# Running the first FFN inside the causal attention, four steps behind it, as one program

## The reference

```python
x = x + attn_a(layernorm(x))    # 16 heads of 8, causal; three heads weight a third of the keys by 1.6
x = x + ffn(layernorm(x))
x = x + attn_b(layernorm(x))    # 16 heads of 8, rotary q and k, no mask
x = x + ffn(layernorm(x))

# ffn: 128 -> 512 -> 512 -> 512 -> 128, ternary weights times a scale per row
h = silu(lin(x, w1)) * lin(x, w2)
h = gelu(lin(h, h1)); h = gelu(lin(h, h2)); y = lin(h, w3)
```

## Time and profile before

| what | us |
|---|---|
| median of 3 runs | 2510.14 |
| lowest and highest | 2504.98 and 2511.56 |
| profiled execution, its own time | 2512.21 |
| its span, first to last instruction | 2510.5 |

### The profile page before, as it was taken

One profiled execution on the slowest core, in us unless ns is written; L12 is line 12 of the kernel. 1 busy time (PEld: TensorE's weight loads), 2 busy tenths in 40 slices (PEclk: granted clock), 3 DMA queues, 4 the chain that ended last, 5 costly groups with the idle time before them and its releaser, 6 DMA issues. The chain is left out here.

```text
span 2510.5 us, 37314 instructions
## 1 busy us (share of the span) xinstructions
PE 2132.8 (85%) x13378; PEld 978.4 (39%) x13378; DVE 1729.4 (69%) x2590; ACT 1482.9 (59%) x2980; POOL 982.5 (39%) x1184
## 2 busy tenths in 40 slices
PE   0889999898996899999379889989998885999998
PEld 0323333233331677777112222222222211777776
DVE  5766777677670666665189899989989833667663
ACT  0265656666663556655127777777777772665655
POOL 2344555454542344554323232323323200544544
PEclk8688988889895899999659999999999986999999
DMA  6243534334331000000323423443343300000000
GB/s 172 64 99 66 114 69 93 85 79 103 66 66 20 1 1 1 1 1 1 75 51 66 104 64 66 88 89 66 67 104 67 66 15 10 8 10 14 13 10 17
DMA packets 99853, 136.48 MB, mean 54 GB/s; under 512 B 20560, under 2 KB 81488, under 8 KB 93520
## 3 DMA queue, kind: packets, MB, share of 16 engines
q1 hardware_dynamic: 99664, 134.02, 24.5%
HBM read 67.91 MB, written 55.57 MB: 49 GB/s over the span
## 5 line engine op out<-in xcount | busy, mean ns | idle before, releaser
L576 DVE TENSOR_REDUCE b_negmax<-ps_max 128x2 f32<-128x1024 f32 x512 | 611.5, 1219 | 97.5 <-PE ps_max L693 95.4
L660 ACT ACTIVATE b_prob<-ps_score 128x512 f32<-128x512 f32 x1024 | 547.7, 598 | 206.8 <-PE ps_score L679 205.6
L660 ACT ACTIVATE a_prob<-ps_score 128x512 f32<-128x512 f32 (+3 forms) x1024 | 384.5, 437 | 259.4 <-PE ps_score L679 256.8
L576 DVE TENSOR_REDUCE a_negmax<-ps_max 128x2 f32<-128x256 f32 (+3 forms) x512 | 410.9, 821 | 178.8 <-PE ps_max L697 173.6
L679 PE MATMUL ps_score<-b_stack_q,stack_k 50*128 50x512 bf16 x1024 | 263.5, 396 | 54.6 <-ACT b_prob L660 46.1
L714 PE MATMUL ps_out<-b_prob,b_v_aug 128*9 128x512 f32 x2048 | 277.7, 615 | 18.3 <-ACT b_o_raw L633 12.5
L493 POOL TENSOR_SCALAR_AFFINE_SELECT a_prob<-a_prob 128x512 f32<-128x512 f32 x256 | 162.5, 635 | 320.9 <-ACT a_prob L660 320.7
L974 PE MATMUL ps_score<-fb_h,w_hi 128*128 128x512 f32 x1024 | 251.9, 401 | 29.8 <-DVE fb_h L888 28.8
L974 PE MATMUL ps_score<-fa_h,w_hi 128*128 128x512 f32 x1024 | 251.5, 400 | 29.7 <-DVE fa_h L888 28.7
L693 PE MATMUL ps_max<-stack_k,b_stack_q 48*128 48x512 bf16 x1024 | 233.5, 396 | 40.6 <-issue 23.8
L679 PE MATMUL ps_score<-a_stack_q,stack_k 50*128 50x512 bf16 (+3 forms) x1024 | 202.2, 330 | 37.5 <-DMA a_stack_q<-a_nm_rows 30.6
(11 more groups left out here) (139 smaller groups left out, 2961.1 us busy)
## 6 DMA issues: line engine op xcount, KB each, us to landing
stack_k<-d_stack SPq DMA_DIRECT2D x64, 384.0 KB, 5.9
d_stack<-a_parts SPq DMA_DIRECT2D x64, 192.0 KB, 4.1
a_stack_q<-d_stack SPq DMA_DIRECT2D x32, 384.0 KB, 5.5
d_stack<-b_parts SPq DMA_DIRECT2D x64, 192.0 KB, 3.7
b_stack_q<-d_stack SPq DMA_DIRECT2D x32, 384.0 KB, 5.5
d_stack<-a_parts SPq DMA_DIRECT2D x64, 128.0 KB, 3.6
d_stack<-b_parts SPq DMA_DIRECT2D x64, 128.0 KB, 3.4
d_stack<-a_parts SPq DMA_DIRECT2D x64, 64.0 KB, 3.7
```

The source lines that it names most:

```text
L576: dve.tensor_reduce(m["negmax"][:, t, :, p], dve_banks("max", k)[:, :, 0:keys], AX.X, ALU.max, negate=True).then_inc(s["max"], 1)
L660: act.activation(m["prob"][u % PROBS][:, g, lo:S], act_bank("score", 4 * u + g)[:, 0:S - lo], ACT.Exp).then_inc(s["prob"], 1)
```

## The change

The causal attention and the first FFN become one stage, `layer`, with one loop of 20 steps. In step n the FFN works on batch n-4 (`FFN = 4`), whose attention ended in step n-1: the output projection moves one step up, to batch n-3 in unit 11. The FFN's work is put into units: turn of the norm in unit 0, gates in units 2 to 5, the hidden layers as blocks behind units 7 and 12, the output layer in unit 14 and its turn in unit 15. In the blocks no scores are made; a maximum stands after each slice. Outside them a unit has one maximum, in eight of the units two. A batch is no longer in its gates while another is in its hidden layers: one batch goes through all of the FFN in one step. The banks stay three and two pairs, and their turns now include the FFN's.

To make room in SBUF there are two stacks instead of three and three buffers of probabilities instead of four. The stacks are loaded in halves of four pairs of heads, the first as soon as the scores of the batch two steps before have passed that half. The gates' low parts go from DVE to POOL; the gates' products are made in place. Norm statistics and xhat of batch n+1 are made in units 10 and 13 of step n. The memsets that put ones into `stack_k` go from the setup into each attention stage. The rotary attention and the second FFN stay as they are but for that and for the flag and half scales, which are now made once, in `layer`. PE's program of the fused stage is written three times (steps 0 and 1, then with and without low weights from step 2).

Cut to its core:

```diff
...
+HALF_LOADS = 4 * 16
...
+SECOND_MAX = (7, 8, 9, 10, 12, 13, 14, 15)
+HIDDEN_UNIT = {2: 7, 3: 12}
+HIDDEN_MAXES = 4
+GATE_UNIT = (2, 3, 4, 5)
+SLOT = {"xT": 0, "fxT": 0, "q": 1, "nm1": 1, "k": 6, "v": 8, "nm0": 11, "proj": 11, "yT": 14, "y": 15}
+ROTARY_SLOT = {"nm1": 1, "xT": 3, "q": 4, "qr": 5, "k": 6, "kr": 7, "v": 8, "nm0": 10, "proj": 2}
...
+def first_max(u):
+    blocks = sum(HIDDEN_MAXES for at in HIDDEN_UNIT.values() if at < u)
+    return u + sum(1 for v in SECOND_MAX if v < u) + blocks
...
-        for stage in (lambda sem: attention(nc, sem, m, a, "a", causal=True),
-                      lambda sem: ffn(nc, sem, m, a, "fa", None),
-                      lambda sem: attention(nc, sem, m, a, "b", causal=False),
-                      lambda sem: ffn(nc, sem, m, a, "fb", out)):
+        for stage in (lambda sem: layer(nc, sem, m, a, "a"),
+                      lambda sem: attention(nc, sem, m, a, "b"),
+                      lambda sem: ffn(nc, sem, m, "fb", out)):
...
-            for c in range(STACKS):
-                last = dve.memset(m["stack_k"][c][:], 1.0)
-            last.then_inc(zeroed, 1)
...
+def layer(nc, sem, m, a, tag):
...
+    STACKS, PROBS, LAG = 2, 3, 2
...
+    act_turns, dve_turns = [], []
+    for u in range(UNITS):
+        act_turns += [("score", 2, 4 * u), ("score", 2, 4 * u + 1)]
+        dve_turns.append(("max", 1, first_max(u)))
+        if u == SLOT["xT"]:
+            act_turns.append(("xT", 0, 0))
+        if u == SLOT["fxT"]:
+            dve_turns.append(("fxT", FFN, 0))
+        act_turns += [("score", 2, 4 * u + 2), ("score", 2, 4 * u + 3)]
+        if u in GATE_UNIT:
+            dve_turns.append(("gate", FFN, GATE_UNIT.index(u)))
+        if u == SLOT["nm1"]:
+            act_turns.append(("nm1", 2, 0))
+        for name in ("q", "k"):
+            if u == SLOT[name]:
+                dve_turns.append((name, 0, 0))
+        if u == SLOT["v"]:
+            dve_turns.append(("v", 0, 0))
+        if u == SLOT["nm0"]:
+            act_turns.append(("nm0", 1, 0))
+        if u == SLOT["proj"]:
+            dve_turns.append(("proj", 3, 0))
+        if u == SLOT["yT"]:
+            act_turns.append(("yT", FFN, 0))
+        if u == SLOT["y"]:
+            dve_turns.append(("y", FFN, 0))
+        if u in SECOND_MAX:
+            dve_turns.append(("max", 1, first_max(u) + 1))
+        for k, at in HIDDEN_UNIT.items():
+            if u == at:
+                act_turns += [(f"h{k}", FFN, f) for f in range(FT)]
+                dve_turns += [("max", 1, first_max(u + 1) - HIDDEN_MAXES + i) for i in range(HIDDEN_MAXES)]
+    act_turns += [None] * (-len(act_turns) % SCORE_BANKS)
+    dve_turns += [None] * (-len(dve_turns) % 2)
...
+        elif name == "gate":
+            pe.wait_ge(s["h1f"], count(FT, b, k + 1))
...
+            for n in range(STEPS):
+                if on(n, 2):
+                    aug(1, n - 2)
+                if on(n, 3):
+                    numerators(n - 3)
+                if on(n, 0):
+                    store(n, "stored_q", 0)
+                if on(n, 3):
+                    store_reciprocals(n - 3)
+                if on(n, 0):
+                    store(n, "stored_k", 1)
+                if on(n, 3):
+                    spread_reciprocals(n - 3)
+                if on(n, 0):
+                    load(n, "stack_q", "stored_q", 0, 0)
+                    load(n, "stack_k", "stored_k", 1, 0)
+                if on(n, 1):
+                    aug(0, n - 1)
+                if on(n, 0):
+                    load(n, "stack_q", "stored_q", 0, 1)
+                    load(n, "stack_k", "stored_k", 1, 1)
...
+            def gate_low(b, f):
+                pool.wait_ge(s["h1_hi"], count(FT, b, f + 1))
+                pool.tensor_tensor(h[1][:, 1, f], gated[:, f % 2], h[1][:, 0, f], ALU.subtract).then_inc(s["h1"], 1)
+            def hidden_low(b, k):
+                for f in range(FT):
+                    pool.wait_ge(s[f"h{k}_hi"], count(FT, b, f + 1))
+                    pool.tensor_tensor(h[k][:, 1, f], hf[:, f % 2], h[k][:, 0, f], ALU.subtract)\
+                        .then_inc(s[f"h{k}"], 1)
...
+            def gate(b, f):
+                banks = dve_banks("gate", f)
+                dve.wait_ge(s["tanh"], count(FT, b, f + 1))
+                dve.scalar_tensor_tensor(out=gated[:, f % 2], in0=gated[:, f % 2], scalar=1.0,
+                                         in1=banks[:, 0], op0=ALU.add, op1=ALU.mult).then_inc(s["ut"], 1)
+                dve.wait_ge(s["ut"], count(FT, b, f + 1))
+                dve.scalar_tensor_tensor(out=gated[:, f % 2], in0=banks[:, 1], scalar=m["s_gate"][:, f:f + 1],
+                                         in1=gated[:, f % 2], op0=ALU.mult, op1=ALU.mult).then_inc(s["h1f"], 1)
+                dve.wait_ge(s["h1f"], count(FT, b, f + 1))
+                if f == 0:
+                    wait(dve, s["yT_ps"], b)
+                dve.tensor_copy(h[1][:, 0, f], gated[:, f % 2]).then_inc(s["h1_hi"], 1)
...
+            norm_stats(dve, m, s, 0, "")
+            for c in range(STACKS):
+                last = dve.memset(m["stack_k"][c][:], 1.0)
+            last.then_inc(s["unit_rows"], 1)
+            norm_apply(dve, m, s, 0, "")
...
+            def hidden(b, k):
+                for f in range(FT):
+                    act.wait_ge(s[f"l{k}_ps"], count(FT, b, f + 1))
+                    if f >= 2:
+                        act.wait_ge(s[f"h{k}"], count(FT, b, f - 1))
+                    elif k == 3:
+                        act.wait_ge(s["h2"], count(FT, b, f + 3))
+                    else:
+                        wait(act, s["h3"], count(FT, b - 1, f + 3))
+                    act.activation(hf[:, f % 2], act_bank(f"h{k}", f), ACT.Gelu, scale=m["s_col"][:, k, f:f + 1])\
+                        .then_inc(s[f"h{k}f"], 1)
+                    act.wait_ge(s[f"h{k}f"], count(FT, b, f + 1))
+                    if f == 0 and k == 2:
+                        wait(act, s["l3_ps"], count(FT, b))
+                    act.activation(h[k][:, 0, f], hf[:, f % 2], ACT.Copy).then_inc(s[f"h{k}_hi"], 1)
...
+                for n in range(first, end):
+                    for u in range(UNITS):
+                        if on(n, 2):
+                            scores(n, u, 0)
+                        if on(n, 1):
+                            maxes(n, first_max(u))
+                        attention_middle(n, u)
+                        if u == SLOT["fxT"] and on(n, FFN):
+                            pe.wait_ge(s["f_xhat"], n - FFN + 1)
+                            dve_banks_free(pe, n, "fxT")
+                            turn(dve_banks("fxT")[:, 0], lambda t: m["f_xhat"][:, t, :]).then_inc(s["f_xT_ps"], 1)
+                        if on(n, 2):
+                            scores(n, u, 1)
+                        if u in GATE_UNIT and on(n, FFN):
+                            gates(n, GATE_UNIT.index(u))
+                        attention_end(n, u)
+                        if u == SLOT["yT"] and on(n, FFN):
+                            output(n)
+                        if u == SLOT["y"] and on(n, FFN):
+                            pe.wait_ge(s["yT"], n - FFN + 1)
+                            dve_banks_free(pe, n, "y")
+                            turn(dve_banks("y")[:, 0], lambda t: yT[:, P * t:P * (t + 1)]).then_inc(s["y_ps"], 1)
+                        if u in SECOND_MAX and on(n, 1):
+                            maxes(n, first_max(u) + 1)
+                        if u < LAG and on(n, 3):
+                            weigh(n - 3, UNITS - LAG + u)
+                        if u >= LAG and on(n, 2):
+                            weigh(n - 2, u - LAG)
+                        for k, at in HIDDEN_UNIT.items():
+                            if u == at:
+                                for f in range(FT):
+                                    if on(n, FFN):
+                                        hidden(n, k, f)
+                                    if on(n, 1):
+                                        maxes(n, first_max(u + 1) - HIDDEN_MAXES + f)
...
+            steps(False, 0, 1)
+            pe.wait_ge(s["halved"], 2)
+            pe.transpose(m["ps_out"][0:1, 0:P], m["flags"][:], m["ident"][:]).then_inc(s["flag"], 1)
+            steps(False, 1, 2)
+            pe.wait_ge(s["halved"], 4)
+            has_low = pe.value_load(m["flag"][:], min_val=0, max_val=1)
+            with pe.If(has_low):
+                steps(True, 2, STEPS)
+            with pe.Else():
+                steps(False, 2, STEPS)
...
+def attention(nc, sem, m, a, tag):
...
+            for c in range(STACKS):
+                last = dve.memset(m["stack_k"][c][:], 1.0)
+            last.then_inc(s["unit_rows"], 1)
...
-                dve.tensor_scalar(s_half[:], m["s_col"][:, 0], 0.5, None, ALU.mult).then_inc(s["halved"], 1)
-                dve.wait_ge(s["halved"], 1)
-                dve.tensor_tensor(s_gate[:], s_half[:], m["s_col"][:, 1], ALU.mult)
```

(46 more changed lines are left out.)

721 lines of the change are left out of this document (557 added, 164 removed).

## The result

The changed kernel takes 2762.0 us, median of four runs (2728.2 to 2764.2), against 2510.9 for the kernel before on the same chip: a ratio of 1.097, with a 95% interval of 1.088 to 1.106. The forecast was 2567 with a range of 2450 to 2690. The sign was right; the loss is 251 us where 55 was forecast.

The account below looks back on a forecast made before the run. The prediction took PE's queue as the bound: 55 us of work plus 15 waiting made a 70.0 us full step. 2512.2 + 44 (fused stage) + 12 (rotary fills) - 1.4 (second FFN) = 2567 us, range 2450 to 2690.

Parts of the forecast that it names:

- and with it the slow clock, if no other wait does the same: Step's end: the DMA wait (some 2.3 us) should go, and the slow clock behind it (some 3.6 us a step).
- The sum of 70.0 us: Full fused step: 55 us of PE work and 15 waiting, 2.3 us more than the two steps it replaces.
- The rival: Waits of 2.3 us behind blocks halve the clock: one fall a step gives 2625 us, two 2683; chance 0.19.
- The lengths laid by hand: Full step: units 0-1 6.4 us, 2-7 19.6, block 9.2, units 8-12 15.6, second block 9.2, units 13-15 10.6.
- So the first full step begins at 197: Start of the fused stage: step 4, at 189.6 us before, begins 7 us later because two stack fills move.
- The end: Last steps of the fused stage: step 16 takes 68 us, step 17 57, steps 18 and 19 some 45 each.
- the 1252 forecast: End of the fused stage: 197 + 840 + 68 + 57 + 90 = 1252 us, against 1208.2 before, so +44.
- 10.6 were forecast: After the fused stage: three rotary stack fills add 12 us, the second FFN's dropped halves and flag save 1.4.
- The table loads: Fused stage: 64 loads of 1.28 us, those into GELU hidden, those back to Exp exposed behind each hidden block.
- The last low part: Last gate's low part on POOL: ready some 27.2 us into the step, when PE asks at 27.4; hidden.
- The rival of 62 us a step, elastic waits: Full step: 8 of the 15 us of waits are absorbed, giving 62 us a step and 2455 us; chance 0.28.
- priced at 3.6 us by subtraction: Causal step before: 44.4 - 2.2 - 28.1 - 10.5 leaves some 3.6 us a step for the slow clock.

Follow-up runs that it names:

- the filled version: The changed kernel with overwritten matmuls ahead of the four longest PE waits of a full step (units 2, 8, 12, 13): 2650.5 us, 1.055 of before.
- The kernel without FFN: The changed kernel with the first FFN's work and norm left out, the fused order kept: 2291.8 us, one run.
- the kernel before with two matmuls: The kernel before with two overwritten matmuls of 512 columns ahead of the DMA wait at each causal step's start: 2465.2 us, 0.985 of before.
- the tanh version: The changed kernel with Tanh in place of GELU in the first FFN only, so no table loads inside the fused stage: 2633.3 us, one run.
- the version filled behind the blocks: The changed kernel with overwritten matmuls only at units 8 and 13, behind the two hidden blocks: 2657.5 us, one run.

## Why the prediction was wrong where it was

**The step that failed: "and with it the slow clock, if no other wait does the same".** The sum of 70.0 us laid every piece at full clock. The same text named the waits that would undo this, of 2.3 us behind each block, gave the case 0.19, and let the sum stand. They came nearly as laid (2.00 and 1.90), were followed by 10.2 and 6.7 us at half clock, and two waits of 1.4 us by 3.4 us each. That is 8.3 us of the step (the filled version), 100 us over twelve steps. The rival had the mechanism right. Its price fits the longest fall (3.5 against 3.6), its count didn't: two falls of 3.6, where four stretches cost 8.3 together. Its 2683 was still 79 us short, for the reasons below.

**The lengths laid by hand** were 3.6 us a step too short, 43 us over twelve steps. With the clock at 1.00 the pieces are 6.6, 20.1, 9.6, 16.2, 9.6 and 11.5, against 6.4, 19.6, 9.2, 15.6, 9.2 and 10.6, and the 0.6 taken off for shorter turns. No piece is far off; all err to the same side. One slice of a block is 2.40 us and was laid at 2.31. The gates were laid 3.4 us apart and came 3.5 apart.

**The start.** "So the first full step begins at 197": its first score stands at 231.6, 34.6 us later.

```profile
231.59 0.61 PE L794 MATMUL ps_score<-a_stack_q,a_stack_k 50*128 50x512 bf16 x2
```

I kept the pace of before for steps 1 to 3, which have no FFN. But they run in the new order too, and take 47, 57 and 55 us from first maximum to first maximum, where before had 38, 42 and 46. The kernel without FFN shows 47, 54 and 55 there and keeps that pace in all its steps. The order itself should have been laid for a step without FFN; the fill of the stacks, the only cost put there, was the smaller one.

**The end.** Steps 16 and 17:

```profile
1213.60:1285.40 71.80, 61.54 (x436) 30.07 (x432) 37.78 (x61) 45.95 (x96) 29.48 (x37) 0.98 0.08 16
1285.40:1358.00 72.60, 58.91 (x304) 27.31 (x300) 14.31 (x30) 45.28 (x95) 28.37 (x33) 0.79 0.05 9
```

Step 16 was laid at 68 and ran at a clock of 0.98, so its 3.8 us more are mostly laid length. Step 17 was laid at 57. It was costed by the maxima it no longer makes, though the waits at blocks and gates, which no maximum causes, stay, and its clock is 0.79. Steps 18 and 19 and the end of the stage took 93.1 us (laid 90).

**The sum of these** is 142.0 for the twelve steps (982.0 us from 231.6 to 1213.6, laid 840), 34.6 for the start, 3.8 and 15.6 for steps 16 and 17 and 3.1 behind them: 199.1, by which the stage ended later than the 1252 forecast. What follows the stage came 7.7 us longer than before (1310.0 against 1302.3), where 10.6 were forecast. That leaves 196, which is the 251 found less the 55 forecast.

**Right.** The table loads: 1.28 us each, exposed only behind the blocks. (The Trainium skill, "ScalarE: Activation LUTs", What ACT_TABLE_LOAD costs, adds a drain of about 1380 ns for each switch. The rows above leave it 0.02 us in front of the exponential and 0.01 us behind the copy; here the measurement decides.) 58 loads stand in the stage, 57 of them for the FFN; 64 were forecast, since steps 18 and 19 have no exponentials to load back for. The DMA wait of a step went. The gates go at the pace of the previous gate's products. The last low part was ready when PE asked: in the full steps PE waits nowhere for POOL. The rotary fills cost 12, of which 9.8 were shown. The rival of 62 us a step, elastic waits, was far from what came.

**Its own gain was misjudged too.** The clock fall that the change was to remove was priced at 3.6 us by subtraction, and put into every step. Filled, it was worth 3.4 to 3.8 for each of the eleven steps that had one, but 2.5 to 2.8 on the average of 15. And it could be had in the kernel before with two matmuls, without moving the FFN.

## What to carry to other kernels

Price a wait of TensorE with the clock behind it: here the waits of 1.9 and 2.0 us of a full step cost 2.4 and 3.5 us more in the work that followed, and those of 1.4 us 0.9 and 1.5. A sum made at full clock has to name every such wait and pay for it. One row in which the clock survives a wait doesn't clear the next one of that length. Where such a wait can't be removed, overwritten matmuls in it give the clock back at almost no cost: 2.8 us a step in the kernel before, 8.3 in the changed one. The dose has to be measured, since too much is work in the path. And when two stages are interleaved, lay the new order once with one of them left out: what it loses alone (9.0 us on 43.7 here) is lost in every step, the first and last ones too.

## What the runs showed of the hardware

- The length of one wait alone doesn't tell whether the clock falls. Waits of 1.4 us were followed by 3.4 us at half clock once in each full step of the tanh version and in seven of eleven of the version filled behind the blocks, and by nothing in the other four. Without the FFN's work no wait was longer than 1.4 between 314 and 630 us, and the clock there was 0.88. In step 16 of the changed kernel a wait of 2.00 us that ends at 1250.88 and one of 1.41 left it at 1.00:

```profile
1209.10:1277.30 68.20, 57.94 (x425) 27.59 (x424) 37.37 (x59) 44.76 (x93) 28.85 (x36) 1.00 0.10 22
```

- What a stretch at half clock costs: 3.5 us for 10.2, 2.4 for 6.7, 0.9 and 1.5 for 3.4 (the changed kernel against its filled version), 1.5 for 3.4 (the version filled behind the blocks, its two kinds of step).
- Filling a wait with products nobody reads held the clock at 1.00 over 589 us of the changed kernel (364 to 953 us).
- A table load between two ACTIVATEs of different tables had 0.01 us of idle before it and 0.02 behind.
- One overwritten matmul of 0.9 us in a wait of 2.3 gave a clock of 0.97 and two thirds of the gain of two by the end of the stage (28.5 us against 41.8), half of it by the time of the whole (20 against 39).
